# Five instruction lists laid out anew in a two-layer graph network, with one wait of the gather narrowed

## The chip, the core and the metric

The kernel runs on one NeuronCore of one Trainium2 chip. The metric is the device time of the whole kernel in microseconds (us). Three runs of the kernel before took 739.4, 739.52 and 740.95 us; the median, 739.52 us, is what the change is measured against.

## The reference

`x` is 8 batches of 1024 nodes with 128 features in float32, `adj` a 1024x1024 0/1 matrix that is symmetric, has its diagonal set and is nearly empty elsewhere. Two layers follow each other, each on a normalized input:

```python
h = relu(layernorm(x))
# layer 0: 4 heads of 32; a softmax inside each of the 8 chunks of 128 keys, the 8 results added
q, k, v = h @ Wq.T + bq, h @ Wk.T + bk, h @ Wv.T + bv
scores = clip(q @ k.T / sqrt(32), -10, 10); scores = where(adj == 0, -10, scores)
attn = softmax(scores.reshape(..., 8, 128), axis=-1)
out = (attn @ v, summed over the chunks) @ Wo.T + bo + h
x = x + layernorm(out) * gamma + beta
# layer 1: graph attention with one head
h = relu(layernorm(x)); Wh = h @ W
e = leaky_relu(Wh @ a1 [:, None] + Wh @ a2 [None, :], 0.2), -inf where adj == 0
x = x + elu(softmax(e, axis=-1) @ Wh)
```

## The kernel before

The program is written engine by engine. There are five lists (TENSOR, SCALAR, VECTOR, GPSIMD, SYNC), one for each engine. A list gives every step a number, its place, and `in_order` sorts the steps of all eight batches by `b * 9600 + place`. What comes out is the order in which that engine issues its instructions. An engine works strictly down its list: where a step waits for a semaphore, all steps behind it wait as well. Steps of batch b and of other batches lie next to each other in a list, so that layer 0 of one batch runs beside layer 1 of earlier ones. In what follows `exp7.31` is step `exp`, number 31, of batch 7.

Layer 0 of a batch has 32 groups of two heads, and 16 steps of four heads (8 key chunks for each half of the 1024 queries):
- `scores` (TensorE, L1593): two matmuls into two of the four `score` banks. It waits until `probs` of the group two before has read them.
- `exp` (ScalarE, L1240): the exponential in place on 128x1024 numbers.
- `probs` (VectorE, L1391): clip and mask in one operation against `cap`, into one of six `probs` buffers.
- `sums` (L1611) and `context` (L1605): eight matmul instructions each on TensorE, the sums of a chunk's softmax and its product with the values. `log_sum` (L1245) and `inverse` (L1248) on ScalarE turn the sum into a factor.
- `gather` on VectorE (L1415) multiplies the context by that factor. For chunk 0 it writes into `gathered`, for chunks 1 to 7 into one of two buffers `scaled`; `gather` on GpSimd (L1167) then adds `scaled` to `gathered`.
- `project`, three normalizations (`stats_` L1364 and `moments_` L1371 on VectorE, `rstd_` L1122 to L1128 on GpSimd, `apply_` L1228 on ScalarE), `gamma`, `beta`, `residual` and `x1` on GpSimd.

Layer 1 of a batch: `to_row`, `wh` (TensorE), eight `peaks` (VectorE, L1458), `row_shift` (GpSimd), `near_row` and `base_row` (TensorE, L1673), 16 `leaky` (VectorE, L1475), 16 `hide` (GpSimd L1192; the odd ones of batches 6 and 7 on VectorE, L1480), 16 `gat_exp` (ScalarE, L1305), eight `share` (TensorE, L1683; in batch 7 L1569), then `invert` (VectorE, L1490), `below` (L1314), `above` (L1323), `exp_below` (L1328) on ScalarE, `add_x1` (L1197) and `add_below` (L1202) on GpSimd, and `store_out`. In batches 6 and 7 (LATE) `to_row` and `near_row` go to `score` banks, so their layer 1 comes after the last `probs` of batch 7.

SyncE issues the transfers (`load_x`, `store_h`, `load_residual`, `store_x1`, `load_x1`, `store_out`), and `stack_query` and `stack_key` (L1042), four transfers each, which spread queries and keys over the partitions before the scores can start. In the text `stack_query5.1` is the second half of the queries of batch 5.

PSUM has four `score` banks, `ctx_ps` for the context, `near` for `near_row`, and two banks `work` for all the rest. The two `work` banks are taken in strict turn by TensorE's order (`turn_of(...) % 2`), and a turn waits until the one before in its bank has been read. In batch 7 the shares go chunk by chunk: each half is a block of 32 products, four for each `gat_exp`, in the order in which ScalarE's list has them, and the last two quarters go to `score` banks. Their end (`above`, `x1`, `below` of quarters 2 and 3, L1523 to L1534) stands on VectorE behind everything else.

Of the kernel before, what the change touches and what calls it, by code (L numbers as in the profile page):

```python
# [12 lines left out]
P = 128  # L13
# [15 lines left out]
PAIR = 2  # L29
# [10 lines left out]
PLACES = 9600  # L40
SCALED = 2
# [3 lines left out]
TENSOR = ({}, {  # L45
    0: {
        "scores": [3387, 3663, 3953, 3956, 4243, 4364, 5013, 5163, 5367, 5560, 5987, 6033, 6357, 6383, 6502, 6550,
            6756, 6972, 7147, 7369, 7396, 7792, 8050, 8227, 8692, 8877, 9156, 9175, 9551, 9610, 10017, 10100],
        "context": [4321, 4930, 5937, 6300, 6447, 6509, 6810, 7389, 7605, 8028, 8487, 9066, 9544, 9925, 10174, 10697],
        "sums": [4195, 4450, 5219, 5736, 6297, 6388, 6645, 6998, 7464, 7897, 8341, 9043, 9359, 9733, 10113, 10609],  # L50
        "turn_x": [1372, 2191],
        "query": [1697, 3958],
        "key": [1810, 3687],
        "value": [2153, 2820],
        "project": [7787, 12797],
        "turn_hidden": [12194, 16090],
        "to_row": [14218, 16285],
        "wh": [17719, 18060, 18275],
        "near_row": [20684, 22739],
        "base_row": [21130, 21654],  # L60
        "share": [24154, 24420, 24839, 24844, 27885, 28370, 29170, 29448],
        "mask": [791, 1553, 1986, 2164, 2711, 2849, 3222, 3679],
        "weights": [2371, 3352],
        "bias_row": [3317],
    },
    1: {
        "scores": [813, 945, 1231, 1341, 1647, 1799, 2231, 2324, 2632, 2903, 3165, 3321, 3781, 3849, 4280, 4342, 4873,
            4993, 5158, 5347, 5717, 5761, 6184, 6374, 6676, 6708, 7051, 7169, 7347, 7482, 8085, 8166],
        "context": [1696, 2098, 2416, 3037, 3812, 4286, 4885, 5149, 5600, 5946, 6622, 6834, 7258, 8077, 8344, 8878],
        "sums": [1444, 1906, 2378, 2989, 3642, 4086, 4468, 5003, 5388, 5894, 6373, 6894, 7388, 8055, 8250, 8676],  # L70
        "turn_x": [-4956, -3281],
        "query": [-4463, 1257],
        "key": [-2260, -556],
        "value": [-422, 935],
        "project": [7770, 12369],
        "turn_hidden": [11964, 17240],
        "to_row": [17366, 17552],
        "wh": [20340, 20699, 20707],
        "near_row": [21676, 23507],
        "base_row": [21265, 22817],  # L80
        "share": [23780, 24287, 25787, 25812, 28248, 28448, 29666, 29915],
    },
    2: {
        "scores": [-1056, -920, -571, -490, -435, -328, 254, 462, 832, 983, 1197, 1299, 1459, 1691, 1953, 2013, 2158,
            2436, 2718, 2824, 2956, 3759, 4407, 4540, 5058, 5413, 5630, 5685, 6105, 6683, 6798, 6953],
        "context": [-428, 436, 519, 1276, 1410, 1814, 2018, 2921, 4427, 4740, 5414, 5671, 6197, 6902, 7535, 7885],
        "sums": [-453, 399, 487, 1145, 1345, 1759, 2345, 3336, 4021, 4389, 4664, 5415, 6106, 6794, 7279, 7711],
        "turn_x": [-9631, -7604],
        "query": [-6967, -532],
        "key": [-4403, -2512],  # L90
        "value": [-2480, -417],
        "project": [8438, 13384],
        "turn_hidden": [11463, 16713],
        "to_row": [16986, 17387],
        "wh": [20672, 20866, 20963],
        "near_row": [21467, 23460],
        "base_row": [21557, 23324],
        "share": [24322, 25129, 25729, 26108, 28457, 28753, 29390, 29685],
# [1625 lines left out]
```

## Time and profile before

| | |
|---|---|
| median of 3 runs | 739.52 us |
| profiled execution, its span | 739.8 us |
| first `exp` / last `probs` done | 31.2 us / 654.5 us |
| mean granted TensorE clock | 0.974 |

The profiled execution is 0.3 us above the median. The page gives the busy time of each engine: it counts from the start of an instruction to its end, overlaps within an engine counted once. "Idle before" is the time that an engine sat still just before an instruction, with what released it. A view by windows gives the same for stretches; three stretches are used below: the head (up to the first exponential of scores), the middle (up to the last `probs` of batch 7) and the tail.

### The profile page before, as it was taken

Reading aid. Unit: us, or ns where it says so; the run is one execution under the profiler, and the core shown is the slowest. Engines: PE = TensorE matmul, PEld = TensorE weight load, DVE = VectorE, ACT = ScalarE, POOL = GpSimd, SP = SyncE. Lnnn points to the kernel's source line nnn. Section 1 sums busy time; section 2 is a strip of 40 time slices with the busy share of each in tenths; the row PEclk is TensorE's granted clock in tenths of the full one; section 3 lists DMA queues with packets and bytes.
Section 4 is the critical chain, followed back from the end, with each engine's and each line's share of the span. In section 5 each row is a group of like instructions: output and inputs, shape, how many; then the busy total and the mean of one; then the engine's idle time right before and its main releaser. Section 6 shows DMA issues by size and latency. Waiting matters only on the chain. (4 is left out here: it accounts for less than half of the span.)

```text
span 739.8 us, 13611 instructions
## 1 busy us (share of the span) xinstructions
PE 667.7 (90%) x4393; PEld 349.7 (47%) x4393; DVE 658.3 (89%) x1165; ACT 660.1 (89%) x1140; POOL 523.2 (71%) x629
## 2 busy tenths in 40 slices
PE   3899999999899998999999998999989998993975
PEld 2523333343344553646344563556436563562865
DVE  3898988999998999899998999889997999989675
ACT  5799999989999899998999999998999899977555
POOL 2165546364778788887878888677887798889553
PEclk9899999999999999999999998999999999998978
DMA  8642242321312142231420424121321312021111
GB/s 282 218 170 100 86 149 87 121 73 58 115 58 82 62 142 86 74 107 38 156 98 32 144 89 140 72 77 39 113 88 72 114 64 67 1 73 43 37 36 44
DMA packets 58647, 68.53 MB, mean 93 GB/s; under 512 B 5328, under 2 KB 35024, under 8 KB 58576
## 3 DMA queue, kind: packets, MB, share of 16 engines
q1 hardware_dynamic: 57568, 67.39, 27.2%
q8 instruction: 36, 0.59, 0.3%
q10 hardware_dynamic: 1008, 0.26, 0.2%
q14 instruction: 35, 0.29, 0.1%
HBM read 21.50 MB, written 12.58 MB: 46 GB/s over the span
## 5 line engine op out<-in xcount | busy, mean ns | idle before, releaser
L1391 DVE SCALAR_TENSOR_TENSOR probs<-score,cap 128x1024 f32<-128x1024 f32 x256 | 308.2, 1215 | 20.3 <-ACT score L1240 19.1
L1240 ACT ACTIVATE score<-score 128x1024 f32<-128x1024 f32 x256 | 257.5, 1014 | 13.6 <-PE score L1593 11.3
L1593 PE MATMUL score<-query_stack,key_stack 128*128 128x512 f32 x512 | 191.0, 459 | 15.8 <-DVE probs L1391 14.5
L1167 POOL TENSOR_TENSOR gathered<-gathered,scaled 128x512 f32<-128x512 f32 x112 | 149.2, 1332 | 48.3 <-DVE scaled L1415 46.2
L1192 POOL TENSOR_TENSOR ring<-ring,see_t 128x512 f32<-128x512 f32 x112 | 132.5, 1193 | 23.9 <-DVE ring L1475 23.4
L1593 PEld LDWEIGHTS score<-query_stack,key_stack 128*128 128x128 f32 x512 | 80.6, 192 | 142.8 <-DVE probs L1391 100.4
L1611 PE MATMUL work<-probs,ones 128*32 128x512 f32 x1024 | 137.0, 609 | 5.6 <-DVE parts L1399 1.2
L1605 PE MATMUL ctx_ps<-probs,value 128*32 128x512 f32 x1024 | 135.4, 600 | 4.7 <-DVE gathered L1415 2.1
L1683 PE MATMUL work<-wh,ring 128*128 128x130 f32 x896 | 110.8, 280 | 9.8 <-ACT ring L1305 9.8
L1683 PEld LDWEIGHTS work<-wh,ring 128*128 128x128 f32 x896 | 107.9, 194 | 21.9 <-issue 15.9
L1305 ACT ACTIVATE ring<-ring,wh 128x512 f32<-128x512 f32 x128 | 88.4, 721 | 8.0 <-DVE ring L1480 4.3
L1415 DVE TENSOR_TENSOR scaled<-ctx_ps,inverse 128x512 f32<-128x512 f32 x112 | 76.3, 681 | 14.2 <-ACT inverse L1248 9.7
L1245 ACT ACTIVATE inverse<-work 128x512 f32<-128x512 f32 x128 | 76.4, 597 | 8.0 <-PE work L1611 7.3
L1248 ACT ACTIVATE inverse<-inverse 128x512 f32<-128x512 f32 x128 | 80.6, 632 | 1.7
L1475 DVE SCALAR_TENSOR_TENSOR ring<-near,wh,to_row 128x512 f32<-128x512 f32 x96 | 69.5, 741 | 0.1
L1458 DVE CUSTOM_DVE_ANT_0 near_row<-to_row,see 128x1024 f32<-128x1024 f32 x48 | 64.2, 1336 | 0.4 <-issue 0.2
L1605 PEld LDWEIGHTS ctx_ps<-probs,value 128*32 128x32 f32 x1024 | 25.5, 108 | 65.5 <-issue 58.9
L1125 POOL TENSOR_TENSOR small<-small,minus_half 128x4 f32<-128x4 f32 x48 | 49.9, 1039 | 3.8
L1611 PEld LDWEIGHTS work<-probs,ones 128*32 128x32 f32 x1024 | 22.4, 109 | 56.6 <-issue 33.3
L1122 POOL TENSOR_TENSOR small<-small,eps 128x4 f32<-128x4 f32 x48 | 13.3, 278 | 43.7 <-DVE small L1371 43.2
L1197 POOL TENSOR_TENSOR gat_out<-gat_out,gat_x 128x256 f32<-128x256 f32 x30 | 26.1, 868 | 18.8 <-ACT gat_out L1323 18.8
L1621 PE MATMUL work<-h_t,w_t 128*128 128x512 f32 x64 | 36.4, 655 | 0.8 <-ACT h_t L1280 0.5
(119 smaller groups left out, 840.0 us busy)
## 6 DMA issues: line engine op xcount, KB each, us to landing
query_stack<-parts SPq DMA_DIRECT2D x64, 256.0 KB, 2.5
key_stack<-parts SPq DMA_DIRECT2D x56, 256.0 KB, 2.5
x_in<-in_x SPq DMA_DIRECT2D x16, 256.0 KB, 3.1
h_kept<-x_in SPq DMA_DIRECT2D x16, 256.0 KB, 2.4
res<-h_kept SPq DMA_DIRECT2D x16, 256.0 KB, 2.8
h<-in_x SPq DMA_DIRECT2D x16, 256.0 KB, 3.3
x_kept<-res SPq DMA_DIRECT2D x16, 256.0 KB, 2.4
gat_x<-x_kept SPq DMA_DIRECT2D x32, 128.0 KB, 2.5
```

The source lines that it names most:

```text
L1167: nc.gpsimd.tensor_tensor(sums, sums, scaled[:, k % SCALED], ALU.add).then_inc(gathered_step, 1)
L1192: nc.gpsimd.tensor_tensor(ring[:, k, :], ring[:, k, :], see_t[:, k % CHUNKS, side], ALU.add).then_inc(hidden_done, 1)
L1240: nc.scalar.activation(some, some, ACT.Exp, scale=DH ** -0.5).then_inc(exp_done, 1)
L1245: nc.scalar.activation(inverse[:, k % LOGS], work[:, bank, :], ACT.Ln).then_inc(work_read[bank], 1)
L1248: nc.scalar.activation(inverse[:, k % LOGS], inverse[:, k % LOGS], ACT.Exp, scale=-1.0).then_inc(share_ready, 1)
L1305: nc.scalar.activation(ring[:, k, :], ring[:, k, :], ACT.Exp, bias=ends[:, k % CHUNKS, 3:4]).then_inc(gat_exp_done, 1)
L1391: nc.vector.scalar_tensor_tensor(out=probs[:, group_of(b, k) % KEPT], in0=score[:, h:h + GROUP, :], scalar=LOW, in1=caps.broadcast_to([P, ...
L1415: nc.vector.tensor_tensor(to, ctx_ps[:, :], inverse[:, k % LOGS], ALU.mult).then_inc(context_read, 1)
L1593: last = nc.tensor.matmul(score[:, head, :], key_stack[:, head, chunk * P:(chunk + 1) * P], query_stack[:, head, half * HALF:(half + 1) * ...
L1605: last = nc.tensor.matmul(ctx_ps[h * DH:(h + 1) * DH, :], value[:, chunk, h * DH:(h + 1) * DH], of_head(b, k, h), start=True, stop=True)
L1611: last = nc.tensor.matmul(work[h * DH:(h + 1) * DH, bank, :], ones[:, :], of_head(b, k, h), start=True, stop=True)
L1683: last = nc.tensor.matmul(work[:, bank, part * (SIGNS + D):(part + 1) * (SIGNS + D)], ring[:, half * CHUNKS + jt, k % TILES * P:(k % TILES ...
```

## The change

PSUM banks hold what they held: `ctx_ps`, `near` and the two `work` banks become one tensor `work` of four banks, with the context always in bank 2, `near_row` always in bank 3 and all other turns in banks 0 and 1. The bank of a turn comes from a string BANKS with one digit for each turn, so that 0 and 1 need not alternate: of 317 turns in them 74 take the same bank as the turn before. The first transposes of the weights go to bank 3, where they went to `ctx_ps`. Semaphores follow: each bank has `work_done` and `work_read`, which take the place of `context_done`, `context_read` and `near_done`.

All five lists have new places. Of TensorE's common steps 496 of 747 stand elsewhere in the order, 1.3 places away in the mean and 18 at most; of ScalarE's 714 of 929 (2.6, 29), of VectorE's 599 of 789 (2.2, 37), of GpSimd's 314 of 405 (2.1, 32), of SyncE's 107 of 158 (1.6, 8). The same operations are issued on the same engines. Three stretches of the lists, read out as orders:

```
ScalarE, start
before: cast0.0 apply_x0.0-1 first_weights mask0.0 turn_x0.0 cast0.1 mask0.1 query0.0 key0.0 mask0.2 cast0.2 value0.0
        mask0.3 turn_x0.1 weights0.0 mask0.4 cast0.3 value0.1 mask0.5-6 weights0.1 exp0.0-1 key0.1 mask0.7 exp0.2-3
after:  apply_x0.0 first_weights cast0.0 turn_x0.0 mask0.0-1 cast0.1 query0.0 key0.0 apply_x0.1 mask0.2 value0.0 cast0.2
        turn_x0.1 mask0.3-4 weights0.0 cast0.3 value0.1 mask0.5 exp0.0 mask0.6-7 exp0.1 weights0.1 exp0.2 query0.1
ScalarE, end
before: base_row7.0-1 gat_exp7.0-13 below7.0 above7.0 gat_exp7.14-15 below7.1 exp_below7.0-1 above7.1 below7.2
after:  base_row7.0-1 gat_exp7.0-9 below7.0 above7.0 gat_exp7.10 exp_below7.0 gat_exp7.11-12 below7.1 gat_exp7.13-14
        above7.1 gat_exp7.15 exp_below7.1 below7.2-3
GpSimd, tail
before: rstd_y7.1 hide6.0 add_below5.3 hide6.2 hide6.4 gamma7.1 hide6.6 hide6.8 x17.1
after:  rstd_y7.1 hide6.0 hide6.2 beta7.1 hide6.4 hide6.6 gamma7.1 x17.1 hide6.8
SyncE, batch 5
before: store_out2.1 load_x12.3 load_x7.0 store_out2.2 stack_query5.1 load_x7.1 store_x14.0
after:  store_out2.1 store_h6.1 load_x13.0 store_out2.2 store_x14.0 load_x7.0 store_out2.3 stack_query5.1
```

In batch 7 the shares are steps of their own in the list (`chunk`, 16 of them, in the order of their numbers), and `near_row7.1` stands between the fourth and the fifth. The last operations on VectorE are steps too, quarter 2 whole before quarter 3.

The wait of VectorE's `gather` (L1415) for GpSimd's additions: chunk 0 waits for none of them, where it waited for all seven of the half before; chunk 2 waits for the addition that frees its buffer.

```diff
-                    wait(dve, gathered_step, b * 14 + 7 * half + max(chunk - SCALED, 0))
-                    dve.wait_ge(context_done, step_of(b, k) + 1)
+                    if chunk:
+                        wait(dve, gathered_step, b * 14 + 7 * half + (-1 if chunk == SCALED else max(chunk - SCALED, 0)))
+                    bank = bank_of(name="context", k=k, b=b)
+                    wait_written(dve, "context", k, b)
                     dve.wait_ge(share_ready, step_of(b, k) + 1)
-                    nc.vector.tensor_tensor(to, ctx_ps[:, :], inverse[:, k % LOGS], ALU.mult).then_inc(context_read, 1)
+                    nc.vector.tensor_tensor(to, work[:, bank, :], inverse[:, k % LOGS], ALU.mult
+                                            ).then_inc(work_read[bank], 1)
...
 def bank_of(name, k, b):
-    return turn_of(name, k, b) % 2
+    return BANK_OF[first_of(name, k, b)]
...
+                elif name == "chunk":
+                    half, n = k // CHUNKS, k % CHUNKS
+                    if k == 0:
+                        free_bank("share", 0, b)
+                        free_bank("share", PAIR, b)
+                    if k == CHUNKS:
+                        pe.wait_ge(probs_ready, group_of(BATCHES, 0))
+                    pe.wait_ge(gat_exp_done, b * 2 * CHUNKS + k + 1)
+                    for t in range(TILES):
...
-                    pe.wait_ge(probs_ready, group_of(b, STEP_GROUPS * (k + 1)))
-                    wait(pe, context_read, step_of(b, k))
```

## Rows read from the trace of the kernel before

**Rows 1.** The page's part 1: busy us, share of the span, instructions.
```profile
PE 667.7 (90%) x4393; PEld 349.7 (47%) x4393; DVE 658.3 (89%) x1165; ACT 660.1 (89%) x1140; POOL 523.2 (71%) x629
```
**Rows 2.** Busy time by windows: stretch, its length, each engine, granted clock, DMA.
```profile
0.00:31.20 31.20, 15.51 (x96) 10.61 (x97) 17.81 (x51) 19.38 (x34) 4.74 (x24) 0.97 0.78 265
...
404.50:491.50 87.00, 82.83 (x548) 43.71 (x544) 78.98 (x139) 82.26 (x147) 69.74 (x78) 0.96 0.31 100
...
654.50:739.80 85.30, 58.67 (x426) 52.48 (x425) 64.31 (x135) 49.93 (x113) 54.92 (x72) 0.86 0.16 45
...
31.20:654.50 623.30, 593.51 (x3874) 286.59 (x3873) 576.20 (x981) 590.80 (x996) 463.56 (x534) 0.99 0.27 90
```
**Rows 3.** Waits in 32:654 us: who waited for whom, total us, times, longest.
```profile
DVE probs L1391 <- ACT score L1240: 19.1, 42, 1.8
DVE scaled L1415 <- ACT inverse L1248: 9.7, 12, 1.9
DVE gathered L1415 <- ACT inverse L1248: 3.4, 3, 1.3
...
ACT score L1240 <- PE score L1593: 11.3, 28, 0.9
ACT gat_below L1314 <- DVE gat_inverse L1490: 6.4, 9, 1.2
ACT inverse L1245 <- PE work L1611: 5.9, 11, 0.9
```
**Rows 4.** Timeline of the head, ScalarE, then GpSimd: start, us, instruction, idle before.
```profile
9.73 1.04 ACT L1335 CAST ring<-probs 128x1024 bf16<-128x1024 int32 x1 [7.65 <-DMA probs<-in_adj]
...
27.51 1.94 ACT L1339 COPY ring<-work 128x1024 bf16<-128x1024 bf16 x2
30.13 0.16 ACT L1355 COPY w<-work 128x2 f32<-128x2 f32 x1 [0.68 <-PE work L1701]
...
31.19 1.93 ACT L1240 ACTIVATE score<-score 128x1024 f32<-128x1024 f32 x2 [0.76 <-PE score L1593]
...
7.20 0.20 POOL L1128 TENSOR_TENSOR small<-small 128x4 f32<-128x4 f32 x1
```
**Rows 5.** Timeline of the tail around batch 6's shares: GpSimd, then TensorE.
```profile
675.49 1.18 POOL L1202 TENSOR_TENSOR gat_out<-gat_out,gat_below 128x256 f32<-128x256 f32 x1
...
679.31 1.71 POOL L1155 TENSOR_TENSOR res<-res,rows 128x512 f32<-128x512 f32 x1
...
683.65 9.48 PE L1683 MATMUL work<-wh,ring 128*128 128x130 f32 x64 [9.77 <-ACT ring L1305]
```
**Rows 6.** Timeline of the last 13 us: ScalarE, GpSimd, VectorE.
```profile
728.15 1.34 ACT L1305 ACTIVATE ring<-ring,wh 128x512 f32<-128x512 f32 x2
...
730.49 0.65 ACT L1323 ACTIVATE gat_out<-work,gat_inverse 128x128 f32<-128x128 f32 x2
...
730.39 0.73 POOL L1202 TENSOR_TENSOR gat_out<-gat_out,gat_below 128x256 f32<-128x256 f32 x1 [1.24 <-ACT gat_below L1328]
...
733.90 0.61 DVE L1523 TENSOR_SCALAR gat_out<-score,gat_inverse 128x128 f32<-128x128 f32 x2 [2.49 <-DMA out<-gat_out]
735.32 0.61 DVE L1523 TENSOR_SCALAR gat_out<-score,gat_inverse 128x128 f32<-128x128 f32 x2 [0.81 <-DMA out<-gat_out]
```
**Rows 7.** Timeline around `stack_query5.1`: SyncE, GpSimd's `add_below2.3`, TensorE's `scores5.16`.
```profile
437.75 2.50 SPq L1042 DMA_DIRECT2D query_stack<-parts  x4
...
436.35 0.73 POOL L1202 TENSOR_TENSOR gat_out<-gat_out,gat_below 128x256 f32<-128x256 f32 x1
...
446.93 0.71 PE L1593 MATMUL score<-query_stack,key_stack 128*128 128x512 f32 x2
```
**Rows 8.** Groups by line: `peaks` from SBUF, and from PSUM (batches 6 and 7).
```profile
L1458 DVE CUSTOM_DVE_ANT_0 near_row<-to_row,see 128x1024 f32<-128x1024 f32 x48 | 64.2, 1336 | 0.4 <-issue 0.2
...
L1458 DVE CUSTOM_DVE_ANT_0 near_row<-score,see 128x1024 f32<-128x1024 f32 x16 | 19.6, 1223 | 4.6 <-PE score L1647 2.7 <-DVE peak L1458 1.5 <-issue 0.2
```

More of the change, by code:

```diff
@@ L40 @@
 PLACES = 9600
+BANK_COUNT = 4
+FIRST_BANK = 3
 SCALED = 2
@@ new lines @@
+    1: {
+        "turn_x": [-6222, -5232],
+        "query": [-5910, -559],
+        "key": [-4410, -2289],
+        "value": [-1993, -964],
+        "scores": [-1009, -876, -605, -472, -308, -132, 31, 240, 536, 582, 935, 1069, 1232, 1408, 1658, 1829, 2087,
+            2197, 2486, 2618, 2870, 2963, 3214, 3291, 3620, 3821, 3955, 4206, 4384, 4636, 4799, 5050],
+        "sums": [-417, -77, 339, 724, 1124, 1550, 1884, 2252, 2673, 3018, 3404, 4010, 4440, 4691, 5114, 5846],
+        "context": [-241, 131, 428, 812, 1299, 1713, 1978, 2348, 2762, 3106, 3492, 4098, 4854, 5278, 5512, 5934],
+        "project": [4548, 9964],
+        "turn_hidden": [8727, 12661],
+        "to_row": [12870, 13166],
+        "wh": [15319, 15730, 15844],
+        "near_row": [16300, 17976],
+        "base_row": [16596, 16777],
+        "share": [18399, 18617, 19338, 19557, 21407, 21579, 22136, 22517],
+    },
@@ L759, in in_order @@
     return [item[1:] for item in sorted(found, key=lambda item: item[0])]
-IN_WORK = ("turn_x", "query", "key", "value", "project", "turn_hidden", "to_row",
-           "wh", "near_row", "base_row", "share", "mask", "weights", "bias_row", "sums")
+IN_WORK = ("turn_x", "query", "key", "value", "project", "turn_hidden", "to_row", "wh", "near_row", "base_row",
+           "share", "mask", "weights", "bias_row", "sums", "context")
 def in_work(name, b, k=0):
-    if name == "share" and b == BATCHES - 1 and k >= TILES:
-        return False
-    return name in IN_WORK and name != "near_row" and not (name == "to_row" and b in LATE)
@@ L773 @@
[L773 to L782 removed]
+    return name in IN_WORK and not (b in LATE and name in ROWS)
@@ new lines, in turns, with first_of @@
+def turns():
+    for name, k, b in in_order("tensor"):
+        if name == "chunk":
+            if k == 0:
+                yield "share", 0, b
+                yield "share", PAIR, b
+        elif in_work(name, b, k) and not (name == "share" and k % PAIR):
+            yield name, k, b
+BANK_OF, COUNT_OF = {}, {}
+for turn, bank in zip(turns(), (int(digit) for digit in BANKS), strict=True):
+    BANK_OF[turn] = bank
+    COUNT_OF[turn] = list(BANK_OF.values()).count(bank)
+def first_of(name, k, b):
+    return name, k // PAIR * PAIR if name == "share" else k, b
```

1439 lines of the change are left out of this document (729 added, 710 removed).

## The prediction

> **What bounds the kernel now.** I read the page's busy times first, then the windows, then the waits, then the timelines of the two ends. The page shows three engines within two per cent of each other: TensorE 667.7, ScalarE 660.1 and VectorE 658.3 of 739.8 us [rows 1]. No engine alone is the bound, and none is full. The windows say where they aren't [rows 2]. In the head (31.2 us) ScalarE works 19.4 us. In the tail (85.3 us) VectorE works 64.3 and ScalarE 49.9. In the middle (623.3 us) ScalarE works 590.8, so it is idle 32.5; TensorE's matmuls fill 593.5, VectorE works 576.2 and is idle 47.1, GpSimd 463.6. Batch 5, with both layers under way, is the same picture: ScalarE 82.3 of 87.0 us, VectorE 79.0 [rows 2].
>
> What remains idle in the middle is many short waits. VectorE's `probs` waits for the exponential 42 times (19.1 us, 1.8 at most) and its `gather` for the factor 15 times (9.7 and 3.4 us). ScalarE's `exp` waits for the scores 28 times (11.3 us), `below` for the inverted sums 9 times (6.4) and `log_sum` for the sums 11 times (5.9) [rows 3]. Each partner had other work ahead in its own list at that moment, for all three engines are over 92% busy. So the idle time is that of three orders which don't quite mesh, and an order can cure it. That is what the change touches, since it issues the same operations on the same engines.
>
> The Trainium skill ("Perfetto Trace Analysis", section Identifying the Most-Contended Engine) says that matmul busy time is no measure of how close TensorE is to its limit, and that the busy share of its weight loads (47% here) is a better one. By that rule TensorE has room, ScalarE is the bound, and the floor of the middle is 590.8 us; taken by matmul busy time it would be 593.5. The sum below is the same by either, only its lower end moves by 2.7 us.
>
> **The change part by part.** The sum is made against the span of 739.8 us; the median of the runs is 0.3 us below it, which I take off at the end.
>
> Bank handling: nothing by itself. The context keeps a bank of its own, `near_row` too, and counts on new semaphores replace old ones. What 74 turns out of strict alternation change is when TensorE may begin; that is in the middle's figure.
>
> The narrower wait: VectorE's `gather` of chunk 0 no longer waits for seven additions. In the trace all idle time before it, 3.4 us in 3 places, is put down to ScalarE's factor and none to GpSimd [rows 3]. Behind a GpSimd wait would stand VectorE's whole list, but that wait isn't there. The gain is 0, and 3.4 us at most if the inference of the releaser is wrong. Chunk 2's wait comes behind chunk 1's on the same engine, which asks for more, so it gives nothing in either case.
>
> Head: ScalarE does nothing but load tables until 9.73 us, since its list begins with a cast that waits 7.65 us for the adjacency. The scale and shift of batch 0 are ready at 7.20 + 0.20 = 7.4 us [rows 4]. The new list begins with `apply_x0.0`, so ScalarE starts 9.73 - 7.4 = 2.3 us earlier. It also moves `mask0.6` behind the first exponential, half of 1.94 us, and `weights0.1`, 0.16 us and two as short behind it, after a wait of 0.68, about 0.9 together [rows 4]: 1.9 us less ahead of the first exponential. ScalarE idles 31.2 - 19.4 = 11.8 us in the head, and 7.65 of it is the first wait; of the other 4.1 I take a quarter, 1.0. Together 5.2 us: the first `exp` at 26.0. The bounds are 2 us (the stacks of query and key then set the start) and 7. What was put off must be done later: 1.3 us of ScalarE's work go into the middle.
>
> Middle: it can't be shorter than ScalarE's work, 590.8 + 1.3 = 592.1 us. So the most that an order can take out is 31.2 us, and the least is nothing or less. Where between? Three in-order engines over 92% busy can't mesh without loss: semaphores take their time, and instruction times vary. On the other hand the named waits are nearly all under 2 us, and steps move by 1 to 3 places in the mean, which is the size needed to cure such waits. I take half of ScalarE's idle time, 16.2 us, less the 1.3: the middle gets 14.9 us shorter. This is the largest and least certain term; no row shows how well the new orders mesh. The low end is a gain of 29, the high end a loss as described among the rivals.
>
> Denser work on VectorE meets GpSimd more often. `peaks` that read both operands from SBUF take 1336 ns, those that read one from PSUM 1223 [rows 8]; over the 48 in SBUF that is 48 x 0.113 = 5.4 us at stake, and a new order can bring more or less of it: 0, with 5.4 both ways for the range. The Trainium skill ("SBUF — State Buffer", section SBUF: two separate sides) has an exclusive lock of the port pair that VectorE and GpSimd share, taken by VectorE's instructions with two SBUF inputs. By that rule a denser middle would lengthen just these instructions and GpSimd's additions; the difference of 113 ns agrees with it.
>
> Tail: two places. First, TensorE waits 9.77 us for batch 6's `gat_exp` before its shares, at 683.65 [rows 5], and behind that block stand `turn_hidden7.1` and `to_row7`, for which VectorE's `peaks7.0` waits. `gat_exp6.7` hangs on `hide6.6` on GpSimd. Ahead of that stood `add_below5.3` (1.18) and `gamma7.1` (1.71) [rows 5]; now `beta7.1` stands there, which is an operation of the same size as `gamma7.1` and takes some 1.3 to 1.7 us. That is 1.2 to 1.6 earlier; 1.5 taken. Second, the end: VectorE's last reads wait 2.49 us and 0.81 for `store_out` of quarters 0 and 1 to free `gat_out` [rows 6]. `below7.0` and `above7.0` now stand behind `gat_exp7.9`, not `gat_exp7.13`, so the first of these stores is long done and the 2.49 us go. What is late next is quarter 1: the last `gat_exp` ends at 728.15 + 1.34 = 729.5; `above7.1` goes ahead of it now (0.65), then come `exp_below7.1` and `add_below7.1` (0.73), the store and its landing. The chain for quarter 3 ends some 2 us earlier. Together 3.5 us, bounds 1 and 6. TensorE's clock in the tail is 0.86 of full speed against 0.99 in the middle [rows 2]; its long wait there hardly shrinks, so I count no gain in clock.
>
> The sum: 739.8 - 0.3 - 5.2 - 14.9 - 3.5 = 715.9, rounded 716 us.
>
> **The rivals.**
> - *The orders mesh almost fully.* The middle comes down to ScalarE's work: 739.5 - 5.2 - 29.9 - 3.5 = 701. For it: 590.8 of 623.3 is reached already. Against it: VectorE and TensorE would both have to follow without a gap of their own.
> - *The waits only change places.* The middle keeps its idle time and takes the 1.3 us; only head and tail gain: 739.5 - 5.2 + 1.3 - 3.5 = 732. For it: the lists keep their overall structure and the steps move little. The same cycle of scores, `exp` and `probs` over four banks stays.
> - *Transfers for the scores get stuck behind layer 1's output: slower.* In SyncE's list `stack_query5.1` now stands behind `store_x14.0` and `store_out2.3`, which waits for `add_below2.3` on GpSimd. Before, that addition ended at 436.35 + 0.73 = 437.1, the stack was issued from 437.75 to 440.25, landed some 2.5 us later, and `scores5.16` ran at 446.93 [rows 7]: about 4 us of slack. If the addition slips by more than 4 us against the scores, each further us stops TensorE's scores, then ScalarE and VectorE. Once costs little. To outweigh the 7.4 us that the second rival gains over before, the slips must reach some 12 us over 4 in sum, in batches 3 to 7, whose stacks lie beside layer 1; with 14 us the time is 732 + 14 = 746. For it: GpSimd's times vary, and the list is now fitted tightly. Against it: the slack is 4 us where I could read it.
> - *It does nothing it can be measured by.* Gains at the ends given back in the middle: 739.5.
>
> **How the numbers follow.** Forecast (706 to 725) 0.46; meshing almost fully 0.13; waits only change places 0.20; no change 0.04; slower 0.17. A difference of 0.2% is about what this measurement can tell from none, so "same" is 738 to 741. Faster: 0.46 + 0.13 + 0.20 = 0.79; same 0.04; slower 0.17. The range leaves out some 0.06 below and 0.14 above: 700 to 740. It takes in the bounds of the head, of the tail, and 5.4 us either way.
>
> **What the profile after would show.** Head: ScalarE's first work at 7.4 us, the first `exp` near 26 us. Middle: from first `exp` to last `probs` about 608 us, ScalarE 97% busy there, the waits of `probs` for `exp` and of `exp` for scores down to about half. `gather`'s idle time as before with no GpSimd in it. Tail: TensorE's wait before the shares of batch 6 shorter by 1.5 us, no wait of over 1 us before the first of VectorE's last reads. The prediction is wrong in its main step if the middle is still over 618 us, and wrong in sign if SyncE's `stack` transfers are issued late and idle time of TensorE's scores is put down to them.

## The result, and the profile after

The kernel after takes 732.8 us (median of 4 runs, 731.54 to 733.93), the kernel before in the same job 739.46: a ratio of 0.9909 [0.9889, 0.9928]. That is 0.9% faster, 6.7 us, clear of noise and inside the range, but the forecast was 23.5 us. The three stages are cut as in the prediction: to the first `exp`, from there to the end of the last `probs`, and the rest.

| us | head | middle | tail | span |
|---|---|---|---|---|
| before | 31.2 | 623.3 | 85.3 | 739.8 |
| forecast | 26.0 | 608.4 | 81.8 | 716.2 |
| after | 38.1 | 609.2 | 83.5 | 730.8 |

The middle is what was forecast. The head is 12 us off, and with the wrong sign. Of the 16.8 us between 732.8 and the forecast of 716, 12.1 are the head, 1.7 the tail and 0.8 the middle; the rest is the difference between spans and medians. The spans differ by 9.0 us and the medians by 6.7: in the runs of this study the time lies some 1.7 us above its span, so the profiled execution of before was one of its longer ones. A second look at the same five lists (run b_narrow below) has 29.7, 620.6 and 85.4 us; against that one the change gives -11.4 in the middle, +8.4 in the head and -1.9 in the tail.

Page of after, part 1, which answers [rows 1], then the windows (stretch, its length, each engine, granted clock, DMA), which answer [rows 2]:
```profile
PE 660.3 (90%) x4393; PEld 350.0 (48%) x4393; DVE 664.4 (91%) x1165; ACT 654.5 (90%) x1140; POOL 526.3 (72%) x629
```
```profile
0.00:38.10 38.10, 16.79 (x85) 11.47 (x85) 15.90 (x49) 18.34 (x30) 12.25 (x27) 0.82 0.72 248
38.10:647.30 609.20, 584.24 (x3884) 285.88 (x3884) 583.74 (x986) 584.57 (x997) 457.63 (x530) 1.00 0.27 91
647.30:730.80 83.50, 59.29 (x424) 52.68 (x424) 64.79 (x134) 51.63 (x116) 56.44 (x74) 0.86 0.16 47
```
In the middle ScalarE works 584.6 us, 96% of it. It is 24.6 us idle, not 32.5, and it also works 6.2 us less, on the same 997 instructions to one. In the head it works 18.3 of 38.1 us: the added time is idle. The first `exp` moves a little from run to run: the profiled executions of the kernels below that have the head of before show 29.7 to 31.2 us, those that have the head of after 36.7 to 38.1. So the head is 5.5 to 8.4 us longer, and a change of 1 us in it means nothing.

Waits of after in 38:647 us, which answer [rows 3] (who waited for whom, total us, times, longest):
```profile
ACT score L1295 <- PE score L1642: 12.8, 33, 1.3
DVE probs L1450 <- ACT score L1295: 10.9, 29, 1.5
DVE scaled L1476 <- ACT inverse L1305: 3.2, 7, 0.8
ACT inverse L1302 <- PE work L1659: 1.4, 6, 0.5
```
Four of the six waits of [rows 3] shrank to a third or less: `gather` for the factor 9.7 to 3.2 (its chunk 0 3.4 to 0.2), `below` 6.4 to 0.2, `log_sum` 5.9 to 1.4. `probs` for `exp` went from 19.1 to 10.9. `exp` for the scores did not shrink: 11.3 to 12.8.

**The head.** Timeline of after: SyncE's issues (start, us, what), then VectorE, ScalarE and TensorE (the bracket is the idle time before, and what ended it).
```profile
12.57 0.43 SPq L1115 DMA_DIRECT2D h_kept<-x_in  x1
22.31 0.38 SPq L1112 DMA_DIRECT2D x_in<-in_x  x1
22.73 0.50 SPq L1129 DMA_DIRECT2D res<-h_kept  x1
23.27 0.43 SPq L1130 DMA_DIRECT2D h<-in_x  x1
23.75 2.92 SPq L1097 DMA_DIRECT2D query_stack<-parts  x4
26.72 0.83 SPq L1115 DMA_DIRECT2D h_kept<-x_in  x1
27.59 2.96 SPq L1097 DMA_DIRECT2D key_stack<-ring  x4
```
```profile
25.09 0.87 DVE L1422 BATCH_NORM_STATS2 small<-x_in 128x6 f32<-128x128 f32 x4 [5.96 <-DMA x_in<-in_x]
...
7.72 1.65 ACT L1283 ACTIVATE x_in<-x_in,small 128x128 f32<-128x128 f32 x4 [5.64 <-POOL small L1183]
...
26.40 1.04 ACT L1393 CAST ring<-ring 128x1024 bf16<-128x1024 int32 x1 [5.74 <-DVE see L1585]
...
36.32 0.59 ACT L1325 COPY value<-work 128x512 f32<-128x512 f32 x1 [5.14 <-PE work L1617]
...
38.08 1.02 ACT L1295 ACTIVATE score<-score 128x1024 f32<-128x1024 f32 x1
...
33.38 1.19 PE L1642 MATMUL score<-query_stack,key_stack 128*128 128x512 f32 x2 [4.01 <-DMA key_stack<-ring]
```
ScalarE does begin at 7.7 us, as forecast. But SyncE, having issued `store_h0.0` by 13.0, stands still until 22.31: `load_x1.0` needs the buffer that this store reads, and the store lands at 22.24. Behind it in the list stand both stacks of batch 0, so `key_stack` is issued at 27.59, where before it was issued at 21.13. The scores wait for it until 33.38, the values of the second half come behind the scores on TensorE, and ScalarE waits for these until 36.32. Meanwhile VectorE has `stats_x1.0` ahead of its `see` steps and stands 5.96 us for the same `load_x1.0`; ScalarE's cast waits 5.74 for that.

### The profile page after: what moved, and what is told of

It reads as the page before. It is cut to its first block, busy times and chain, and to the rows that moved or that the text cites. A ratio compares the mean times of both kernels' runs of the same rounds, so it can differ in the third digit from the quotient of the medians.

```text
span 730.8 us, 13599 instructions
## 1 busy us (share of the span) xinstructions
PE 660.3 (90%) x4393; PEld 350.0 (48%) x4393; DVE 664.4 (91%) x1165; ACT 654.5 (90%) x1140; POOL 526.3 (72%) x629
## 4 chain that ended last, share of the span: by engine, by line
PE 38%; DVE 23%; ACT 14%; issue 10%; POOL 8%; DMA 4%; SPq 3%; DVEq 0%; POOLq 0%; ACTq 0%
DVE probs L1450 11%; PE work L1725 11%; PE score L1642 9%; PE work L1659 7%; PE work L1653 6%; ACT score L1295 5%; DVE ring L1541 3%; POOL ring L1247 2%; DVE scaled L1476 2%; DVE near_row L1520 2%; SPq L1097 2%; PE work L1617 1%; DMA h_kept<-x_in 1%; ACT ring L1363 1%; ACT inverse L1302 1%
## 5 line engine op out<-in xcount | busy, mean ns | idle before, releaser
L1450 DVE SCALAR_TENSOR_TENSOR probs<-score,cap 128x1024 f32<-128x1024 f32 x256 | 307.2, 1215 | 12.3 <-ACT score L1295 10.9
L1295 ACT ACTIVATE score<-score 128x1024 f32<-128x1024 f32 x256 | 258.0, 1016 | 13.7 <-PE score L1642 12.8
L1642 PE MATMUL score<-query_stack,key_stack 128*128 128x512 f32 x512 | 188.0, 452 | 20.5 <-DVE probs L1450 11.1
L1642 PEld LDWEIGHTS score<-query_stack,key_stack 128*128 128x128 f32 x512 | 79.0, 189 | 147.7 <-DVE probs L1450 103.9
L1653 PE MATMUL work<-probs,value 128*32 128x512 f32 x1024 | 134.9, 598 | 3.1 <-DVE scaled L1476 2.6
L1363 ACT ACTIVATE ring<-ring,wh 128x512 f32<-128x512 f32 x128 | 89.0, 721 | 11.1 <-POOL ring L1247 6.9
L1476 DVE TENSOR_TENSOR scaled<-work,inverse 128x512 f32<-128x512 f32 x112 | 76.2, 680 | 5.7 <-ACT inverse L1305 3.2
L1541 DVE SCALAR_TENSOR_TENSOR ring<-work,wh,to_row 128x512 f32<-128x512 f32 x96 | 70.0, 740 | 0.3 <-PE work L1719 0.3
L1520 DVE CUSTOM_DVE_ANT_0 near_row<-to_row,see 128x1024 f32<-128x1024 f32 x48 | 69.6, 1450 | 0.6 <-ACT to_row L1341 0.5
L1653 PEld LDWEIGHTS work<-probs,value 128*32 128x32 f32 x1024 | 26.4, 108 | 68.6 <-issue 31.8
L1177 POOL TENSOR_TENSOR small<-small,eps 128x4 f32<-128x4 f32 x48 | 11.7, 243 | 57.2 <-DVE small L1429 56.9
L1257 POOL TENSOR_TENSOR gat_out<-gat_out,gat_below 128x256 f32<-128x256 f32 x30 | 29.8, 997 | 7.1 <-ACT gat_below L1386 6.4
```

The lines of the kernel that those rows point to most:

```text
L1295: nc.scalar.activation(some, some, ACT.Exp, scale=DH ** -0.5).then_inc(exp_done, 1)
L1363: nc.scalar.activation(ring[:, k, :], ring[:, k, :], ACT.Exp, bias=ends[:, k % CHUNKS, 3:4]).then_inc(gat_exp_done, 1)
L1450: nc.vector.scalar_tensor_tensor(out=probs[:, group_of(b, k) % KEPT], in0=score[:, h:h + GROUP, :], scalar=LOW, in1=caps.broadcast_to([P, ...
L1476: nc.vector.tensor_tensor(to, work[:, bank, :], inverse[:, k % LOGS], ALU.mult).then_inc(work_read[bank], 1)
L1520: nc.vector.tensor_tensor_reduce(out=near_row[:, :], in0=late_row if b in LATE else to_row[:, :], in1=see[:, k, :], scale=1.0, scalar=-3e3 ...
L1541: nc.vector.scalar_tensor_tensor(out=ring[:, k, :], in0=row, scalar=ends[:, j, 2:3], in1=to_row[:, side], op0=ALU.add, op1=ALU.max).then_i ...
```

## The experiments

Steps are named batch.step, as in the prediction; in a few of the expectations the two numbers are swapped, so that `rstd_x0.4` and `gather7.2` are batch 4's first and batch 2's eighth. Each median stands beside runs of the kernel before in the same job: 738.65 for head_sp, head_both, tail_near and both_ends; 738.25 for inv_adjacent, b_inv_apart, gather_early and head_all; 737.64 for b_inv_gather, old_gather2, head_dve and best2; 739.46 for rstd_moved, b_narrow and best3. Since these differ by up to 1.8 us, kernels of different jobs are compared by their ratios where it matters. What the new list of one engine is worth alone, and what the freer choice of bank is worth, no run shows.

### The head: two lists, and a third behind them

head_sp, SyncE's list of the kernel after:
```diff
-store_h0.0, load_x1.0, load_residual0.0, stack_query0.0, store_h0.1, stack_key0.0, load_x1.1
+stack_query0.0, stack_key0.0, store_h0.0, load_x1.0, load_residual0.0, store_h0.1, load_x1.1
```


> The changed kernel with one move in SyncE's list: stack_query0.0 and stack_key0.0 stand ahead of store_h0.0, load_x1.0 and load_residual0.0, as they did before the change. Theory (the 7 us lost in the head come from SyncE: load_x1.0 waits for store_h0.0 to land behind 4 MB of adjacency, and both stacks are queued behind it): the stacks are issued from about 17 to 22 us and land by 25, but VectorE still waits at stats_x1.0 for load_x1.0, which lands at about 25 as now, and ScalarE's cast waits for VectorE behind it. So the first exp comes at about 33.5 us instead of 38.1 and the time is 4.6 us shorter, about 728. Rival (the middle takes it back, since what was late in the head was off the path of a full middle): under 1.5 us, about 732.

Measured 731.01, ratio 0.9896 [0.9881, 0.9911], first `exp` at 37.1, which the untouched head reaches too: a miss. The time is the rival's, not its reason. Timeline of head_sp, SyncE, then VectorE:
```profile
16.63 2.56 SPq L1097 DMA_DIRECT2D query_stack<-parts  x4
19.24 3.06 SPq L1097 DMA_DIRECT2D key_stack<-ring  x4
22.35 0.62 SPq L1115 DMA_DIRECT2D h_kept<-x_in  x1
25.43 0.39 SPq L1112 DMA_DIRECT2D x_in<-in_x  x1
...
28.14 0.87 DVE L1422 BATCH_NORM_STATS2 small<-x_in 128x6 f32<-128x128 f32 x4 [9.53 <-DMA x_in<-in_x]
```
The keys are now issued 8.3 us earlier, but `load_x1.0` 3.1 us later, and VectorE stands 9.53 us before `stats_x1.0`. One brake had covered the other. The row of the store tells one thing more: here the load follows the end of the store's issue (22.97) by 2.5 us, in after by 9.3.

head_dve, VectorE's list alone, SyncE's as in after:
```diff
-cast0.1, stats_x1.0, see0.2, ... cast0.3, bias_row0, moments_x1.0
+cast0.1, see0.2, ... cast0.3, bias_row0, stats_x1.0, moments_x1.0
```


> The changed kernel with only VectorE's part of head_both: stats_x1.0 directly ahead of moments_x1.0. head_sp alone brought the first exp from 38.1 to 37.1 us, both together to 28.8. Theory (two blocks side by side, either of which holds the first exp): alone this brings it to 36 to 38 us, since SyncE's stacks are still issued from 23.7 and land at 33.4; the time is within 2 us of the changed kernel. Rival (VectorE's was the block that counted): the first exp under 32 us, the time 5 us shorter.

Measured 730.75, 0.9902 [0.9887, 0.9918], first `exp` at 36.8, as its theory had it. Alone each of the two edits gives nothing that can be told from the run-to-run spread.

head_both, both edits:

> As head_sp, and stats_x1.0 on VectorE stands directly ahead of moments_x1.0, behind the casts, see and edges of the adjacency. Theory: two in-order lists were blocked by the same late transfer; with both free the first exp comes at 27 to 28 us and the time is about 10 us shorter than that of the changed kernel, 722 to 723. Rival (SyncE alone was the block): the same as head_sp. Rival (the middle takes it back): about 731.

Measured 728.13, 0.9859 [0.9844, 0.9874]; stages 28.8, 614.1 and 83.0. The first `exp` came 9.3 us earlier than in after, where head_sp and head_dve, with one edit each, show 1.0 and 1.3. But the middle grew by 4.9. Waits of head_both in 29:100 us, one row:
```profile
ACT x_in L1257 <- POOL small L1157: 4.2, 1, 4.2
```
ScalarE stands 4.2 us before the normalization of batch 1, since GpSimd's `rstd_x1.0` has `beta0.0` and `residual0.0` ahead of it, and these wait for `load_residual0.0`, which is late now.

head_all moves that step as well, together with the edit of tail_near below:
```diff
 GpSimd
-rstd_x0.0, rstd_x0.1, beta0.0, beta0.1, residual0.0, residual0.1, rstd_x1.0
+rstd_x0.0, rstd_x0.1, rstd_x1.0, beta0.0, beta0.1, residual0.0, residual0.1
```


> both_ends and rstd_x0.1 and rstd_x1.1 on GpSimd ahead of beta0.0 and of gather0.1. In head_both and both_ends the first exp came 9 us earlier, but batch 0 took 4 us longer: ScalarE stood 4.2 us at apply_x1.0 for rstd_x1.0, which GpSimd holds behind beta0 and residual0, and these wait for load_residual. Theory (a third list blocked by the same late transfers): those 4.2 us go and the time is 3 to 4 us under that of both_ends, about 723.5. Rival (batch 0 is slow since the transfers themselves crowd there): within 1 us of both_ends.

Measured 722.75, 0.979 [0.9771, 0.9809]; stages 29.1, 610.7 and 81.6. The wait of 4.2 us is gone from ScalarE's rows. (`rstd_x1.1`, which the expectation names too, already stood ahead of `gather0.1` in after.) So the head is a chain of three lists, and the whole gain takes all three: together, with the edit of the tail, 0.9909 - 0.979 of the time of before, some 9 us.

### The tail

tail_near, TensorE's list:
```diff
-chunk7.0, chunk7.1, chunk7.2, chunk7.3, near_row7.1, chunk7.4
+near_row7.1, chunk7.0, chunk7.1, chunk7.2, chunk7.3, chunk7.4
```


> The changed kernel with near_row7.1 ahead of chunk7.0 in TensorE's list, where the kernel before had it. Theory (in the new list the second half's row waits behind the products of four chunks, and VectorE stands 2.1 us at leaky7.8 for it): that wait goes, the last leaky and the end come 2 us earlier, about 731. Rival (the end is set by ScalarE's and GpSimd's steps for quarter 1 and the stores, not by leaky): no change, 732.8.

Measured 729.26, 0.987 [0.9853, 0.9886], tail 81.5 us, 2.0 less than after. This looks right, but the rows don't bear it out. TensorE's first block of sums over batch 7's chunks, in after, then in head_sp, whose code is the same from here to the end:
```profile
706.21 5.95 PE L1741 MATMUL work<-wh,ring 128*128 128x130 f32 x32 [2.07 <-ACT ring L1363]
...
712.00 0.60 PE L1719 MATMUL score<-eye,row_shift 128*128 128x128 f32 x4
712.43 3.74 PE L1741 MATMUL work<-wh,ring 128*128 128x130 f32 x32
```
```profile
707.33 3.81 PE L1741 MATMUL work<-wh,ring 128*128 128x130 f32 x32 [2.07 <-ACT ring L1363]
```
Windows over the first 3.8 us of that block, after and head_sp (the granted clock is the third number from the end):
```profile
706.20:710.00 3.80, 3.79 (x17) 3.80 (x18) 3.80 (x7) 2.85 (x5) 3.04 (x3) 0.50 0.00 0
```
```profile
707.30:711.10 3.80, 3.77 (x34) 3.80 (x35) 3.80 (x7) 2.85 (x5) 3.04 (x3) 1.00 0.00 0
```
The same 32 matmuls take 5.95 us at a granted clock of 0.50 (1.2 GHz) and 3.81 at 1.00. Ahead of both lies an idle time of 2.07 us. head_sp's tail is 81.7 us with no edit in the tail, so 2 us of tail are this clock's, and tail_near had the full clock. Its block of 64, then that of before and that of both_ends (head_both with this edit):
```profile
706.43 7.51 PE L1711 MATMUL work<-wh,ring 128*128 128x130 f32 x64 [1.51 <-ACT ring L1333]
```
```profile
714.45 9.44 PE L1569 MATMUL work<-wh,ring 128*128 128x130 f32 x64 [1.22 <-ACT ring L1305]
```
```profile
702.41 9.38 PE L1685 MATMUL work<-wh,ring 128*128 128x130 f32 x64 [1.22 <-ACT ring L1307]
```
The half clock is the common case, in before too. Where both kernels had it there, head_both and both_ends, the gain is 0.8:

> head_both and tail_near together. If head and tail are independent of each other and of the middle, the gains add: 10 + 2 = 12 us less than the changed kernel, about 721. If TensorE's clock or the middle takes some back: 724 to 728.

Measured 727.33, 0.9853 [0.9829, 0.9877], against 0.9859 for head_both, within the intervals. The traces narrow it further. From the start of batch 7's first row products (TensorE, `eye,row_shift`) to the end of the span it is 27.0 us in head_sp and 27.0 in tail_near, both at the full clock. At the half clock it is 29.1 to 29.5 in after, head_both, head_dve and rstd_moved, and 28.7 and 29.0 in both_ends and best2. So `near_row7.1` behind chunk 3 costs nothing at the full clock and under 1 us at the half. That tail_near is 2.9 us under after by the ratios is more than this; its four runs have mean clocks of 0.976 to 0.980, three of after's four 0.972 to 0.975, and whether the edit has a part in that is not shown. Of the 6 us that both_ends misses from its 721, head_all gains 4.7 by the ratios with GpSimd's step, found above.

### The middle: how much is ScalarE's own time

A look at why ScalarE works 6.2 us less. Timeline of inv_adjacent, where each `inverse` stands directly behind its `log_sum`; then of after, where something stands between:
```profile
250.68 0.60 ACT L1270 ACTIVATE inverse<-work 128x512 f32<-128x512 f32 x1
251.31 0.63 ACT L1273 ACTIVATE inverse<-inverse 128x512 f32<-128x512 f32 x1
```
```profile
245.91 0.59 ACT L1302 ACTIVATE inverse<-work 128x512 f32<-128x512 f32 x1
246.43 1.01 ACT L1295 ACTIVATE score<-score 128x1024 f32<-128x1024 f32 x1
247.35 0.59 ACT L1341 COPY to_row<-work 128x512 f32<-128x512 f32 x1
```
An instruction that needs nothing of the one ahead starts some 0.1 us before that one's end. One that reads its result starts after it. Over all 128 `log_sum` of after the median from start to start is 0.629 us with its own `inverse` next and 0.480 with anything else. Before had 52 such pairs and after has 11, and 41 x 0.15 = 6.2 us. Undo that in after (117 `inverse` moved up to their `log_sum`):
```diff
-log_sum2.6, exp2.16, gat_exp0.0, inverse2.6
+log_sum2.6, inverse2.6, exp2.16, gat_exp0.0
```


> The changed kernel with each inverse directly behind its own log_sum in ScalarE's list (it is there 11 times of 128 in the changed lists, 52 times before). In both traces a log_sum takes 0.63 us from its start to the next start where its own inverse follows, and 0.48 where anything else does. Theory (the new ScalarE list won the middle in good part by setting the two apart, 41 pairs x 0.15 = 6.2 us of ScalarE's time, which the page counts as busy): 117 pairs more cost 117 x 0.15 = 17.5 us of ScalarE's time, and the kernel gets 12 to 18 us longer. Rival (the early inverse lets gather and context go earlier and pays it back, so adjacency is no loss): within 3 us.

Measured 746.36, 1.0106 [1.0088, 1.0125]: 13.6 us over after, inside the 12 to 18 of its theory. In the profiled execution the middle is 16.0 us longer (625.2), but that isn't all busy time: ScalarE works 595.7 us there, 11.1 more, and idles 29.5, 4.9 more. So a pair costs 0.095 us of busy time, and 41 pairs explain 3.9 of the 6.2 us; that 41 x 0.15 gives just 6.2 is luck. The traces say the same: summed up over the middle, `log_sum` overlaps the instruction behind it by 7.1 us in before and by 10.9 in after. The remaining 2.3 us weren't varied by themselves; other instructions overlap more as well (`exp` 16.6 and 17.9 us). The same thing the other way round, in the kernel before (51 `inverse` one step later):
```diff
-log_sum, inverse, exp
+log_sum, exp, inverse
```


> The kernel before with one part of the change alone: in ScalarE's list 51 of the 52 inverses that follow their own log_sum change places with the step behind them. Theory: ScalarE's list gets 51 x 0.15 = 7.7 us lighter, some of it lost because gather now waits longer for the inverse (0.5 to 0.9 us later each time): 3 to 7 us shorter, about 733 to 736. Rival (only three lists laid out together bring anything; gather's waits take all of it): within 1.5 us of the kernel before or slower.

Measured 760.06, 1.0294 [1.0277, 1.0311]: 22 us slower where 3 to 7 us faster was expected. ScalarE's work in the middle fell by 3.2 us, its idle time rose from 32.5 to 54.1. Waits of b_inv_apart in 40:640 us:
```profile
DVE scaled L1398 <- ACT inverse L1231: 26.6, 35, 1.8
...
ACT score L1223 <- PE score L1576: 26.4, 42, 2.2
```
In before these were 7.2 and 10.6 in the same window. VectorE's `gather` was placed to come 0.70 us (median) behind the end of its `inverse`. With the factor 0.5 to 1 us later it stands still, `probs` behind it is late, and the scores with it. In after the median distance is 1.25 us: the new lists took the pairs apart and moved the `gather` along. Moving it along alone does not do it either:

b_inv_gather, b_inv_apart with 52 `gather` one step later on VectorE:

> b_inv_apart and in VectorE's list of the kernel before the 51 gathers that go with the moved inverses (and one more) change places with the step behind them, in 30 cases a probs. In b_inv_apart the inverses came one step later and gather's waits for them rose from 11 to 30 us; probs, scores and exp behind them lost 21 us. Theory (a shift in one list costs because its partner list was fitted to the old place; shifted together the lists mesh again and ScalarE keeps its 7.7 us): most of the loss is gone, 733 to 742 us. Rival (the context bank and the scaled buffers are held longer by the later gather, so TensorE's context now waits): 750 or more.

Measured 772.78, 1.0477 [1.0454, 1.0499]: worse again by 12.7. Waits of b_inv_gather in 40:640 us:
```profile
PE ctx_ps L1565 <- DVE scaled L1375: 27.4, 31, 1.7
...
ACT score L1200 <- PE score L1553: 37.1, 47, 2.3
```
In before TensorE's context waited 1.5 us for a `gather` into `scaled` to read its bank, here 27.4: there is one bank for it, and each step later on VectorE keeps it longer. And the opposite shift in after, 39 `gather` of batches 1 to 6 one step earlier:
```diff
-probs, gather
+gather, probs
```


> The changed kernel with 39 of VectorE's gather steps of batches 1 to 6 put ahead of the probs that stood directly before them. In the trace of the change gather starts 1.3 us (median) after its inverse is done, before the change 0.7. Theory (the new VectorE list places gather later, so it waits for the inverse 3 us where it waited 13): the waits of gather for the inverse return to 8 us or more, and the kernel gets 3 to 8 us longer. Rival (VectorE's gather has slack and its place doesn't matter): within 1.5 us.

Measured 759.35, 1.0285 [1.0266, 1.0304]: 27 us over after, where 3 to 8 were expected; `gather` waits 16.0 us for the factor and `exp` 32.1 for the scores. So one place on one engine, early or late, costs 0.2 to 0.7 us for each step moved, and the step itself lasts 0.68.

best3 takes 10 of the last 11 pairs apart, in the best kernel (below):

> The best kernel so far with, on ScalarE, 10 of the 11 inverse copies that still stand directly behind their log_sum moved one step later. Theory A, each adjacency left costs 0.15 us of ScalarE's time: 10 x 0.15 = 1.5 us less, 720.0 to 721. Rival B, as in the kernel before, a factor that comes 0.5 us later makes VectorE's gather late and the orders mesh worse: 10 places at (760.1 - 738.3) / 51 = 0.43 us each is 4 us more, about 725 to 727.

Measured 726.18, 0.9816 [0.9796, 0.9836], some 3 us slower than best2 by the ratios. ScalarE's work in the middle fell from 584.8 to 584.0, its idle time rose from 27.2 to 31.7. Rival B.

### The narrower wait

old_gather2, after with the old wait (and one step of GpSimd moved, without which the old wait closes a circle):
```diff
-                    if chunk:
-                        wait(dve, gathered_step, b * 14 + 7 * half + (-1 if chunk == SCALED else max(chunk - SCALED, 0)))
+                    wait(dve, gathered_step, b * 14 + 7 * half + max(chunk - SCALED, 0))
 GpSimd
-rstd_x4.0, gather2.7
+gather2.7, rstd_x4.0
```


> The changed kernel with the old wait of VectorE's gather for GpSimd's additions (chunk 0 waits for all seven of the half before). In these lists that wait closes a circle at one place, so rstd_x0.4 on GpSimd is moved behind gather7.2, eight steps or fewer. Theory (the narrower wait gives no time by itself, since GpSimd's additions are done early; it only makes room for this order at one place): within 1.5 us of the changed kernel. Rival (chunk 0 would wait for GpSimd where VectorE is full): 3 us or more longer, with waits of gathered for GpSimd.

Measured 754.65, 1.0212 [1.0175, 1.0248]: 22 us over after, the rival's outcome. Whether the moved step does it is told by rstd_moved, which has the moved step alone:

> The kernel after, with its narrower wait, and only the one step moved that the run of the old gather wait had moved too: GpSimd's rstd_x0.4 from ahead of gather7.2 to behind it. Theory A, the old wait itself costs the 22 us (VectorE stood 11.3 us in 4 places and 4.7 us in 4 before its gather of chunk 0 there): the moved step costs nothing, time within 2 us of the kernel after (about 731 to 733), no idle time before VectorE's gathered. Rival B, the moved step delays batch 4's rows and causes it: 740 or more, and ScalarE or VectorE idle at x_in of batch 4.

Measured 731.32, 0.9891 [0.9871, 0.9911], no slower than after. So the old wait costs 23.3 us in the new order. VectorE's instructions with output `gathered` in old_gather2, with the idle time before them, then in rstd_moved:
```profile
L1463 DVE TENSOR_TENSOR gathered<-work,inverse x16: 676/691/692, 53.5 to 644.1; 128x512 f32<-128x512 f32 x16
its engine sat idle before it (us, times) until:
  issue: 11.3, 4
  POOL gathered L1210: 4.7, 4
```
```profile
L1464 DVE TENSOR_TENSOR gathered<-work,inverse x16: 656/680/692, 54.2 to 620.0; 128x512 f32<-128x512 f32 x16
its engine sat idle before it (us, times) until:
  issue: 0.5, 1
```
The 11.3 us that have no releaser are GpSimd's too. Batch 5's first chunk in old_gather2, VectorE, then GpSimd:
```profile
430.57 0.69 DVE L1463 TENSOR_TENSOR gathered<-work,inverse 128x512 f32<-128x512 f32 x1 [3.94 <-issue]
...
427.80 2.68 POOL L1210 TENSOR_TENSOR gathered<-gathered,scaled 128x512 f32<-128x512 f32 x2
```
GpSimd's seventh addition ends at 430.48 and the `gather` starts 0.09 later. In after:
```profile
416.63 0.68 DVE L1476 TENSOR_TENSOR gathered<-work,inverse 128x512 f32<-128x512 f32 x1
...
417.90 4.53 POOL L1222 TENSOR_TENSOR gathered<-gathered,scaled 128x512 f32<-128x512 f32 x2
```
There the `gather` starts 5.8 us ahead of the end of that addition. Read so for all 15 first chunks that have a predecessor: in before it starts 0.3 to 7.0 us behind the seventh addition in every one; in after it is ahead in 10 of them, by 24.7 us in sum. In old_gather2 the same 10 start 0.1 us behind the addition, with 18.3 us of idle time before them. The new lists run VectorE past the old wait.

b_narrow, the kernel before with the narrower wait alone:

> The kernel before, its five lists as they were, with the narrower wait of VectorE's gather alone. Theory A, the wait is worth something only together with an order in which VectorE comes early to the first chunk: in the trace of before no idle time stood before it on GpSimd's account, so the time stays within 1.5 us of before (736 to 739.5). Rival B, part of the idle time before the gather that the trace of before puts down to ScalarE's factor was GpSimd's addition: 734 or less, up to 3.4 us faster. Rival C, VectorE goes on earlier and its list comes to other steps in another phase: slower by 5 us or more, as one place's shift did in other runs.

Measured 739.12 (10 runs), 0.9994 [0.9981, 1.0006]: nothing. The four corners, in ratios to before:

| | old wait | narrower wait |
|---|---|---|
| old lists | 1 | 0.9994 |
| new lists (GpSimd's one step moved) | 1.0212 | 0.9891 |

Neither part is worth anything alone. The lists alone (with their banks) make the kernel slower by 2%.

### A kernel that beats both

best2 is head_all with TensorE's first scores moved behind the values of the second half:
```diff
 TensorE
-scores0.0, value0.1, mask0.5
+value0.1, mask0.5, scores0.0
```


> head_all with scores0.0 behind mask0.5 in TensorE's list, so that value0.1 and mask0.5 don't wait behind scores0.0 for key_stack to land. In head_both ScalarE stood 2.3 us at value0.1 for this, just before the first exp. Theory (the head's last in-order block): the first exp at 26.5 us where it was 29.1, and the time 1.5 to 2.5 us under head_all's, about 721. Rival (batch 0's middle takes it back, as it took half of head_both's gain): 722.5.

Measured 721.96 (721.21 to 722.52), 0.978 [0.9763, 0.9798]: 2.2% under before and, by the ratios, 1.3% under after. Its first `exp` is at 25.5 us; its middle is 612.0 and its tail 83.1. Against head_all the gain of 0.8 us is within the intervals, so the rival has it: the first `exp` comes 3.6 us earlier, and middle and tail are 1.3 and 1.5 us longer.

## Why the prediction was right or wrong

- **Head, -5.2 forecast, +6.9 measured: the step that failed.** The prediction costed ScalarE's list alone ("ScalarE idles 31.2 - 19.4 = 11.8 us in the head") and named the stacks of query and key only as a bound of 2 us, as if they came when they did before. The diff moved them behind `store_h0.0`, `load_x1.0` and `load_residual0.0` on SyncE, and `stats_x1.0` ahead of the `see` steps on VectorE. Neither was given a price, though the prediction looked at just such a queue for batch 5. What the runs showed in its place: the first `exp` comes at 38.1 us, since `key_stack` is issued at 27.59 instead of 21.13 and VectorE stands 5.96 us for `load_x1.0`; mended one at a time neither moves it beyond the spread of the runs, both together bring it to 28.8. The start at 26 us was there to be had: best2 has 25.5, with four lists mended.
- **Middle, -14.9 forecast, -14.1 measured (-11.4 against b_narrow).** The size was right, by other parts than the sum gave. Idle time of ScalarE fell by 7.9 us (4.7 against b_narrow), not 16.2 (`below` and `log_sum` wait 10.7 us less, `exp` 1.5 more), and its busy time by 6.2 (6.7) where 1.3 more was put in. Two wrong sizes made up a right sum, which is luck. The "floor" of 590.8 us was none: ScalarE's 584.6 lie below it. The Trainium skill ("Perfetto Trace Analysis", section Identifying the Most-Contended Engine) takes busy time as a fair measure of how close ScalarE and VectorE are to their limit. Here it held about 0.1 us for each of 52 dependent pairs, which is some 4 of the 6.2 us, and an order could take most of that out.
- **"The waits of probs for exp and of exp for scores down to about half".** The first, yes (19.1 to 10.9), the second, no (11.3 to 12.8). Most of the time came from waits that I had counted as the smaller ones.
- **The narrower wait, 0 forecast.** In the old order that is what it is worth. In the new one it is worth 23.3 us. The reasoning "that wait isn't there" read the trace of before for an order that had yet to come; each of the two parts was priced on its own, and they can't be.
- **Tail, -3.5 forecast, -1.8 measured.** TensorE's wait before batch 6's shares is 9.09 us instead of 9.77: 0.7 shorter, not 1.5. VectorE's last reads wait 0.64 instead of 2.49 and 0.81, as forecast. But from batch 7's first row products (709.58 in before, 701.35 in after) to the end it is 30.2 and 29.5 us, 0.8 shorter where 2 were forecast. Both terms were sized too large. TensorE's clock doesn't explain it: at batch 7's first sums before had the half clock too (64 matmuls in 9.44 us; 7.51 in tail_near at the full one).
- **"The waits only change places", 732.** The time measured, 732.8, is this rival's, but by another way: its middle of 625 us with all its idle time did not come, and the head that it counted as a gain was the loss.
- **The slower rival, SyncE's stacks.** For batch 5 it did not happen: `stack_query5.1` was issued at 438.78, 1.0 us later than in [rows 7], and TensorE's scores waited 1.5 us, once, for a query stack in the whole of 40:640 us. Its mechanism was real, and did its harm in the head.
- **Contention on VectorE's memory port.** `peaks` with both operands in SBUF take 1450 ns in after, 1336 in [rows 8]; those with one in PSUM 1221 and 1223.
```profile
L1520 DVE CUSTOM_DVE_ANT_0 near_row<-to_row,see 128x1024 f32<-128x1024 f32 x48 | 69.6, 1450 | 0.6 <-ACT to_row L1341 0.5
L1520 DVE CUSTOM_DVE_ANT_0 near_row<-score,see 128x1024 f32<-128x1024 f32 x16 | 19.5, 1221 | 2.7 <-DVE peak L1520 1.5 <-PE score L1696 0.5 <-issue 0.4
```
  That is 48 x 0.114 = 5.5 us more of VectorE's time, the upper bound of the term. The rule cited in the prediction (the Trainium skill, "SBUF — State Buffer", section SBUF: two separate sides) agrees: only the form with two SBUF inputs grew. It bears on a middle in which VectorE works 583.7 us, as much as ScalarE. No run here prices it by itself.

## What to carry to other kernels

When five in-order lists change at once, walk every list past every moved step up to the first instruction of the loop, DMA queues first: a load that waits for a store's buffer holds all that stands behind it. Price a loosened wait together with the order that goes with it; each alone can be worth nothing or be harmful. In a schedule this tight, don't shift one kind of step on one engine alone: one place cost 13 to 27 us in three trials with 39 to 52 steps each.

## What the runs showed of the hardware that was not expected

- ScalarE overlaps independent instructions by about 0.1 us. One that reads the result of the instruction directly ahead comes 0.15 us later (0.629 against 0.480 from start to start). With 117 more such pairs, 11.1 of the 16.0 us by which the middle grew counted as busy time.
- The load behind `store_h0.0` was issued 9.3 us after that store in after (7.7 to 9.3 in the seven kernels with SyncE's new list), and 2.5 us after it in head_sp, where the store was issued 10 us later. In after the adjacency's last load lands at 18.8 us, the last small load, issued just ahead of the store, at 21.6, and the store at 22.2, 9.7 us after its issue began; in head_sp all of these had landed by 19.8 and the store took 3.0 us. That the transfers ahead of it are what holds the store fits this, but no run has the same store without them.
- TensorE's granted clock behind the same idle time of 2.07 us was 0.50 in after and 1.00 in head_sp, whose code is the same there; the 32 matmuls took 5.95 and 3.81 us. The half clock (5.8 us and more) also stands there in before, head_both, head_dve, rstd_moved, both_ends and best2.
- The mean granted clock can go with the order too. In old_gather2's middle TensorE is busy 592.9 us at a clock of 0.98, against 584.2 at 1.00 in after. Three of its runs took 754.6 to 755.5 us at mean clocks of 0.962 to 0.964, the fourth 749.6 at 0.972. So some 5 of the 23.3 us may go with the clock; how the rest divides was not told apart.
